# A one-core kernel for grouped attention and a mixture of experts: reordered start and passage, and output products in three fp32r parts from block 15

## The chip, the cores and the metric

The kernel runs on one core of a Trainium2 chip, as one launch. The time is the device time of an execution in microseconds (us). A program of one core has no other core to wait for, so this is its own span and what lies around it.

## What is computed

The reference is one pre-normalised layer on x of 8 sequences x 256 tokens x 256 features, all in fp32: attention with 32 query heads and 8 key heads of width 64, and then 8 experts, of which each token uses its 2 best.

```python
B, S, H = 8, 256, 256
NH, NKV, HD = 32, 8, 64
x = x + attn(layernorm(x))
x = x + moe(layernorm(x))

def attn(h):                       # wq, wk are rotated by rope; causal softmax
    q, k, v = h @ wq.T, h @ wk.T, h @ wv.T
    p = softmax(mask(rope(q) @ rope(k).T / sqrt(64)))
    return (p @ v) @ wo.T

def moe(h):
    val, idx = top_k(h @ gate, 2)
    c = softmax(val)               # weights of the two experts
    for e in idx:                  # w0, w1: 256x512, wo: 512x256
        out += c[e] * ((silu(h @ w0[e]) * (h @ w1[e])) @ wo[e])
```

## The kernel before

**Precision.** A matrix product in plain fp32 takes TensorE (PE) several passes. So the kernel splits most operands into two fp32r tiles, `hi` (the value, cast) and `lo` (value minus `hi`), and adds up three products, hi*hi, lo*hi and hi*lo. ScalarE (ACT) makes `hi`, and VectorE (DVE) makes `lo`. The second product of the experts is an exception: `output` multiplies fp32 tiles, 4 products of 128x256 for a block.

**Attention.** The work goes in 64 turns, `turn(b, g)` for batch b and key head g (a group of 4 query heads). Products of the projections land in the bank `x_bank` ("projected" in rows). ACT and DVE move them out: `rope_q` and `rope_k` on DVE multiply by cosine and sine (`by_cos`, `by_sin`, `k_cos`, `k_sin`), GpSimd (POOL) adds the two ("rotated"), and SyncE (SP) issues the DMAs that put the rotated heads into `kT` and `qT`, 4 for a group (`move_k`, `move_q`). SP also loads the projection weights in 20 pieces into 4 raw slots (`load_piece`); a slot is free again when the piece in it has been split (`split_w` on ACT and on DVE). SP's queue is in order: a load that stands behind a move waits for it. At the start, PE makes keys, then group q0, then q1, all in `x_bank`, so each has to wait until DVE has read the one before.

**Routing.** While attention runs, the gate logits, ranks and slots of the tokens are worked out in small steps on all engines, put between the turns and, for the last two batches, between the blocks (`side_work`). `lane_codes_scaled` (ACT) prepares operands of the `pairs` products (PE); `gap_exp` (ACT) is the exponential of the gates' softmax; `choice_weights` (DVE) uses it.

**Blocks.** The tokens, sorted by expert, make 39 blocks of 128 rows (0 to 38), 17 of them early (`EARLY_BLOCKS`), in which only tokens of the first six batches stand. For block j PE does 6 products for h0, 4 transposes of the block before (tg), 6 products for h1, 2 transposes of the next rows (tx), and the output of the block before (yb). Beside it ACT does silu of h0, a copy of tg into `gT` and a cast of tx into `xsT_hi`, and DVE does `gate_rows` (silu times h1), `x_lo` (`xsT_lo`) and `y_scale` (yb times the gate weight). POOL gathers rows and scatters results by indirect DMA. PE takes the block's expert from the tile `owners` into a register (`owner`).

**Weights of the experts** come by DMA in 8 slots of two halves and are split in place: `slot_hi` on ACT, `slot_lo` on DVE, half by half, by `split_half(j)` in the blocks' side work. Block j waits (`slots_ready`) until the slots that it may use are split. A block's `side_work` on DVE stands ahead of its `y_scale` in DVE's order.

## Time and profile before

| what | value |
| --- | --- |
| time, median of 3 runs (all three) | 809.29 us (806.13, 809.29, 809.66) |
| the profiled execution: its time, its span | 808.83 us, 807.0 us |
| mean granted clock of TensorE | 0.988 |
| busy, share of the span | PE 94%, PEld 80%, DVE 63%, ACT 60%, POOL 53% |
| chain that ended last, by engine | PE 78%, DVE 11%, ACT 4%, issue 4%, DMA 1%, SP's queue 1% |
| its largest lines | h 13%, projections 10%, attn_out 10%, probsT 9%, scores 9%, yb 8% |

An engine is busy while an instruction of it runs; PEld is TensorE loading weights, which overlaps PE. The chain is followed back from the last instruction to what released it, step by step, so it says which work set the time. Rows of it say "start us, us, what"; "issue" is time in which the engine waited for nothing that the profile shows. In a timeline the bracket at the end is the idle time before the instruction and who ended it.

### The profile page before, as it was taken

To read this page: it belongs to the slowest core of one execution; us is meant where nothing else is said; L and a number is where in the kernel's file an instruction comes from. 1 tells how busy PE (TensorE), PEld (TensorE's weight loads), DVE (VectorE), ACT (ScalarE), POOL (GpSimd) and SP (SyncE) were. 2 spreads that over 40 slices of the span, in tenths; PEclk is the share of its full clock that TensorE was granted. 3 is DMA by queue.
4 is the path that set the end of the run, shared out by engine and by line. 5 is a ranking of instruction groups with operands and counts; after the bars stand their busy time and mean duration, and the time that the engine had idled before them with its cause. 6 is when DMAs were issued, how large, how long until landed. Compare 5 with 4: busy or idle time off the path is not lost.

```text
span 807.0 us, 19409 instructions
## 1 busy us (share of the span) xinstructions
PE 756.3 (94%) x5952; PEld 643.5 (80%) x5952; DVE 512.3 (63%) x2117; ACT 480.5 (60%) x1537; POOL 424.3 (53%) x674
## 2 busy tenths in 40 slices
PE   3789999999999999999999999998798999999994
PEld 3678898888888889888888888876587778888883
DVE  5688676767757757766775785888665754333331
ACT  2477877776777777777777767768455432222221
POOL 1365665655655556556565555555324545554442
PEclk9999999999999999999999999999999999999998
DMA  6433123303212130231221213025962233222330
GB/s 204 122 108 105 58 64 73 73 32 76 67 34 61 47 75 33 69 71 35 73 67 38 57 41 76 31 66 152 387 208 40 43 51 50 46 39 43 52 52 6
DMA packets 52852, 61.05 MB, mean 76 GB/s; under 512 B 10545, under 2 KB 45617, under 8 KB 52753
## 3 DMA queue, kind: packets, MB, share of 16 engines
q1 hardware_dynamic: 45264, 50.46, 21.3%
q0 software_dynamic: 7488, 9.36, 6.9%
q8 instruction: 51, 0.84, 0.5%
q14 instruction: 49, 0.39, 0.2%
HBM read 26.21 MB, written 9.32 MB: 44 GB/s over the span
## 4 chain that ended last, share of the span: by engine, by line
PE 78%; DVE 11%; ACT 4%; issue 4%; DMA 1%; SPq 1%; POOLq 0%; POOL 0%; DVEq 0%; ACTq 0%
PE h L1610 13%; PE projected L379 10%; PE attn_out L526 10%; PE probsT L486 9%; PE scores L473 9%; PE yb L1629 8%; PE heads_out L505 6%; PE projected L400 3%; PE heads_out L508 3%; PE projected L357 2%; PE tg L1620 2%; ACT exps L601 1%; ACT exps L599 1%; DMA raw<-w_attn 1%; DVE masked L726 1%
## 5 line engine op out<-in xcount | busy, mean ns | idle before, releaser
L976 POOL TENSOR_SCALAR probs<-exps,inv_sums 128x128 f32<-128x128 f32 x256 | 97.3, 380 | 216.9 <-DVE inv_sums L734 169.7
L608 ACT COPY pT<-probsT 128x384 f32<-128x384 f32 x256 | 121.8, 476 | 82.5 <-PE probsT L486 82.4
L599 ACT ACTIVATE exps<-masked,neg_max 128x128 f32<-128x128 f32 x256 | 103.0, 402 | 54.4 <-DVE neg_max L728 54.2
L486 PE MATMUL probsT<-identity,probs 128*128 128x128 f32 x768 | 130.6, 279 | 5.0 <-ACT pT L608 4.8
L601 ACT ACTIVATE exps<-masked,neg_max 128x256 f32<-128x256 f32 x256 | 127.3, 497 | 0.0
L977 POOL TENSOR_SCALAR probs<-exps,inv_sums 128x256 f32<-128x256 f32 x256 | 125.7, 491 | 0.0
L1832 POOL DMA_INDIRECT out<-y,to_token x39 | 61.9, 1587 | 107.4 <-DVE y L1751 85.2
L379 PE MATMUL projected<-xT_hi,w 128*128 128x256 f32 x512 | 113.6, 302 | 4.9 <-DVE k_sin L716 2.5
L1610 PE MATMUL h<-experts_w,xsT_hi 128*128 x312 | 106.8, 424 | 2.3 <-DVE xsT_lo L1741 1.3
L728 DVE CUSTOM_DVE_ANT_0 masked<-scores,tables 128x256 f32<-128x256 f32 x256 | 107.4, 419 | 0.2 <-issue 0.2
L473 PE MATMUL scores<-kT,qT 64*128 64x128 f32 (+1 forms) x1024 | 102.9, 341 | 2.7 <-DMA qT<-rotated 2.7
L486 PEld LDWEIGHTS probsT<-identity,probs 128*128 128x128 f32 x768 | 88.1, 142 | 18.8 <-issue 11.7
L726 DVE CUSTOM_DVE_ANT_0 masked<-scores,tables 128x128 f32<-128x128 f32 x256 | 71.8, 281 | 47.9 <-PE scores L473 40.2
L962 POOL TENSOR_TENSOR rotated<-by_cos,by_sin 128x512 f32<-128x512 f32 x64 | 84.8, 1325 | 20.2 <-DVE by_sin L705 20.2
L379 PEld LDWEIGHTS projected<-xT_hi,w 128*128 128x128 f32 x512 | 85.9, 195 | 8.8 <-DVE k_sin L716 4.0
L473 PEld LDWEIGHTS scores<-kT,qT 64*128 64x128 f32 x1024 | 73.8, 190 | 16.7 <-issue 10.7
L734 DVE RECIPROCAL inv_sums<-sums 128x2 f32<-128x2 f32 x256 | 41.6, 163 | 67.9 <-ACT exps L601 66.1
L1729 DVE TENSOR_TENSOR raw<-h,raw 128x512 f32<-128x512 f32 x39 | 26.9, 691 | 89.8 <-PE h L1610 85.1
L1688 ACT ACTIVATE raw<-h 128x512 f32<-128x512 f32 x39 | 23.3, 598 | 98.7 <-PE h L1610 98.6
L505 PE MATMUL heads_out<-pT,v_all 128*64 128x256 f32 x512 | 81.2, 396 | 0.6 <-ACT pT L608 0.6
L1629 PE MATMUL yb<-experts_w_out,gT 128*128 x312 | 75.8, 386 | 4.1 <-ACT gT L1693 2.9
L379 PE MATMUL projected<-xT_lo,w 128*128 128x256 f32 x256 | 73.6, 287 | 0.0
(181 smaller groups left out, 1626.3 us busy)
## 6 DMA issues: line engine op xcount, KB each, us to landing
qT<-rotated SPq DMA_DIRECT2D x256, 64.0 KB, 2.2
kT<-k_cos SPq DMA_DIRECT2D x64, 128.0 KB, 3.4
experts_w<-w_in SPq DMA_DIRECT2D x16, 512.0 KB, 7.0
raw<-w_attn SPq DMA_DIRECT2D x20, 256.0 KB, 3.3
experts_w_out<-w_out SPq DMA_DIRECT2D x8, 512.0 KB, 7.7
out<-x_all SPq DMA_DIRECT2D x8, 256.0 KB, 2.3
xn_rows<-raw SPq DMA_DIRECT2D x8, 256.0 KB, 3.9
x_all<-x SPq DMA_DIRECT2D x1, 1792.0 KB, 10.5
```

The lines of the kernel that those rows point to most:

```text
L379: mm = nc.tensor.matmul(x_bank[:, a * SEQ:(a + 1) * SEQ], part[:, at:at + P], x[:, b % 2, k, :], start=(i % 6 == 0), stop=(i % 6 == 5))
L473: mm = nc.tensor.matmul(s_bank[2 * pair + odd][:, tt * SEQ:tt * SEQ + (tt + 1) * P], qT[rows, g % 2, pair, tt * P:(tt + 1) * P], kT[rows, ...
L486: mm = nc.tensor.transpose(p_bank[:, at:at + P], probs[:, h, at:at + P], ident[:, :])
L505: mm = nc.tensor.matmul(o_bank[rows, pair * SEQ:(pair + 1) * SEQ], v, pT[:, n % 2, h, 0:2 * P], start=(pair == 0), stop=False, skip_group_ ...
L599: nc.scalar.activation(exps[:, h, 0:P], masked[:, h, 0:P], ACT.Exp, bias=neg_max[:, h, 0:1], scale=-1.0, accum_out=sums[:, h, 0:1])
L601: nc.scalar.activation(exps[:, h, P:3 * P], masked[:, h, P:3 * P], ACT.Exp, bias=neg_max[:, h, 1:2], scale=-1.0, accum_out=sums[:, h, 1:2] ...
L608: nc.scalar.copy(pT[:, n % 2, h, :], p_bank[:, 0:3 * P]).then_inc(pT_done, 1)
L728: nc.vector.tensor_tensor_reduce(masked[:, h, P:3 * P], s_bank[h][:, SEQ:2 * SEQ], mask[:, 0:2 * P], -(HD ** -0.5), 3e38, ALU.add, ALU.min ...
L976: nc.gpsimd.tensor_scalar(probs[:, h, 0:P], exps[:, h, 0:P], inv_sums[:, h, 0:1], 1.0, ALU.mult, ALU.mult)
L977: nc.gpsimd.tensor_scalar(probs[:, h, P:3 * P], exps[:, h, P:3 * P], inv_sums[:, h, 1:2], 1.0, ALU.mult, ALU.mult).then_inc(probs_done, 1)
L1610: mm = nc.tensor.matmul(ps[:, :], x[:, j % RING, k * P:(k + 1) * P], w[:, bass.ds(expert * 2 * WI + part * WI + (which * KT + k) * MLP, MLP)],
L1629: mm = nc.tensor.matmul(yb[:, 0:EMB], gT[:, k * P:(k + 1) * P], w_out[:, bass.ds(expert * WO + k * EMB, EMB)], start=(k == 0), stop=(k == ...
```

## The change

It has five parts.

- **Start.** PE runs 9 products of the identity with itself ahead of the first transposes and 7 ahead of the keys (`keep_busy`). The groups q0 and q1 are made in two other banks (`y_bank`, "attn_out", and `o_bank`, "heads_out"). Weight pieces 0 and 1 are loaded ahead of the cosine tables. ACT's queue, no longer SP's, issues the 4 moves of the first keys (`move_first_keys`). On DVE, both groups' reads come sooner, among `bn_stats` and splits.
- **Passage from attention to the blocks.** `lane_codes_scaled` goes ahead of two exponentials of the last turn, the turn whose projection is "r" makes its query products whole, a one-element silu is put behind the last turn, and block 0's second half of products goes behind the transposes of block 1.
- **Early blocks.** `gap_exp` goes from the side work of block 4 to that of block 6, `choice_weights` from 5 to 7, and `split_half` leaves out block 6, so that each later half is split one block later.
- **Output from block 15 on.** `output_parts` makes 12 fp32r products of 128x256 from `gT_hi`, `gT_lo`, `second_hi`, `second_lo`. For each such block ACT copies the expert's second weights into `second_hi` (128x1024) and makes `gT_hi`, and DVE makes `second_lo` and `g_lo`, ahead of the next `gate_rows`. The four tiles use space of the attention stage, whose tiles `lane_hot`, `block_codes` and `gT` are moved to the shared stage.
- **Owners.** PE reads the next block's owner behind the fourth h0 product of a block, and works out the next weights' addresses among the h1 products. At the passage to block 17 it waits for the late owners first.

The diff, cut to its core:

```diff
         sp.dma_start(ident[:, :], t["ident"]).then_inc(r["ident_in"], 16)
+        load_piece(0)
+        load_piece(1)
         sp.dma_start(tables[:, :], t["attn_consts"]).then_inc(consts_in, 16)
-        for i in range(SLOTS):
-            load_piece(i)
+        load_piece(2)
+        load_piece(3)
         sp.dma_start(x_all[:, TT:TILES, :], x_dram[:, TT:TILES, :]).then_inc(x_rest_in, 16)
-        move_k(0, 0)
+        move_q(0, 0, True)
         load_piece(SLOTS)
         load_piece(SLOTS + 1)
-        move_q(0, 0, True)
         move_q(1, 1, True)
         for i in range(SLOTS + 2, SLOTS + EARLY):
             load_piece(i)
...
+        def keep_busy(n):
+            for i in range(n):
+                nc.tensor.matmul(s_bank[0][:, 0:P], ident[:, :], ident[:, :], start=True, stop=True)
         pe.wait_ge(r["ident_in"], 16)
+        keep_busy(9)
         x_transposes(0)
+        keep_busy(7)
...
-        project_q(0, 1)
+        project_q(0, 0, bank=y_bank)
+        project_q(0, 1, bank=o_bank)
         batches(turn)
...
+            if (b, g) == (LAST, 7):
+                rt["lane_codes_scaled"](act, 0)
             exponentials(b, g, 2)
             exponentials(b, g, 3)
-            if (b, g) == (LAST, 7):
-                rt["lane_codes_scaled"](act, 0)
             copy_probs(b, g, 0)
             if (b, g) == (LAST, 6):
                 rt["slot_hi"](act, 0, 0)
...
-        for i in range(3):
-            split_w(i)
+            if (b, g) == (LAST, 7):
+                nc.scalar.activation(r["sums"][:, 0, 0:1], r["sums"][:, 0, 0:1], SILU)
+        def move_first_keys():
+            act.wait_ge(k_rotated, 1)
+            for a in range(2):
+                for copy in range(2):
+                    at = copy * HD + a * 32
+                    act.dma_start(kT[at:at + 32, 0, :, :], k_cos[:, a, :]).then_inc(k_in[0], 16)
+        split_w(0)
+        split_w(1)
         x_hi(0)
+        split_w(2)
         split_w(3)
+        move_first_keys()
         split_w(4)
         batches(turn)
         out_hi(LAST, KV_HEADS - 2)
...
         rope_k(0, 0)
+        rope_q(0, True, y_bank)
         split_w(2)
         dve.wait_ge(x_rest_in, 16)
-        for i in range(TT, TT + 4):
+        for i in range(TT, TT + 3):
             nc.vector.bn_stats(stats[:, i, :], x_all[:, i, :])
-        rope_q(0, True)
-        for i in range(TT + 4, TT + 7):
+        rope_q(1, False, o_bank)
+        split_w(3)
+        for i in range(TT + 3, TT + 7):
             nc.vector.bn_stats(stats[:, i, :], x_all[:, i, :])
-        rope_q(1)
-        split_w(3)
         for i in range(TT + 7, TILES):
             ins = nc.vector.bn_stats(stats[:, i, :], x_all[:, i, :])
...
     def split_half(j):
-        return (2 + (j - 1) // 2, (j - 1) % 2) if 1 <= j <= 12 else None
+        n = j - 1 if j < 6 else j - 2
+        return (2 + n // 2, n % 2) if 1 <= j <= 13 and j != 6 else None
...
             pe.wait_ge(gated_done, j + 1)
+            if j > THREE_FROM:
+                pe.wait_ge(gT_lo_done, j - THREE_FROM)
             for k in range(MT):
...
+        def output_parts(j, between=None):
+            i = j - THREE_FROM
+            pe.wait_ge(gT_done, j + 1)
+            pe.wait_ge(second_lo_done, i + 1)
+            pe.wait_ge(y_done, j)
+            n = 0
+            for g, part in ((gT_hi, second_hi), (gT_hi, second_lo), (gT_lo, second_hi)):
+                if n == 2 * MT:
+                    pe.wait_ge(gT_lo_done, i + 1)
+                    if between:
+                        between()
+                for k in range(MT):
+                    mm = nc.tensor.matmul(yb[:, 0:EMB], g[:, k * P:(k + 1) * P], part[:, k * EMB:(k + 1) * EMB],
+                                          start=(n == 0), stop=(n == 3 * MT - 1))
+                    n += 1
+            mm.then_inc(yb_ps, 1)
...
         for j in range(1, BLOCKS):
-            last, expert = owner(j - 1), owner(j)
+            last, expert = expert, following
+            def next_owner(n):
+                nonlocal following
+                if n == 3 and j < LAST and j != EARLY_BLOCKS - 1:
+                    following = owner(j + 1)
...
             pe.wait_ge(gated_done, j)
             slots_ready(j)
-            hidden(j, expert, 0)
+            hidden(j, expert, 0, next_owner)
             g_transposes(j - 1)
-            hidden(j, expert, 1)
+            hidden(j, expert, 1, next_addresses)
             if j < LAST:
                 x_transposes(j + 1)
             outputs_ready(j - 1)
-            output(j - 1, last)
+            if j < LAST:
+                output(j - 1, last)
+            if j == EARLY_BLOCKS - 1:
+                pe.wait_ge(rt["owners_late"], 1)
+                following = owner(j + 1)
             if j == 1:
...
+        def last_transposes():
+            g_transposes(LAST)
+        output_parts(LAST - 1, last_transposes)
+        output(LAST, expert)
...
+            if j >= THREE_FROM:
+                act.wait_ge(yb_ps, j)
+                nc.scalar.copy(gT_hi[:, :], tg[:, :]).then_inc(gT_done, 1)
+                return
             nc.scalar.copy(gT, tg[:, :]).then_inc(gT_done, 1)
+        def second_split_hi(j):
+            if j == THREE_FROM:
+                act.wait_ge(r["pairs_done"], 2)
+                act.wait_ge(rt["owners_late"], 1)
+                for place in range(EXPERTS):
+                    act.wait_ge(r["w_out_in"][place], 16)
+            expert = act.value_load(r["owners"][0:1, j:j + 1], min_val=0, max_val=EXPERTS - 1)
+            act.lower_ap(w_out[:, bass.ds(expert * WO, WO)])
+            act.wait_ge(yb_ps, j)
+            nc.scalar.copy(second_hi[:, :], w_out[:, bass.ds(expert * WO, WO)]).then_inc(second_hi_done, 1)
...
-            if j == 4:
+            if j == 6:
                 rt["gap_exp"](act, 1)
...
             if j < LAST:
                 x_copy(j + 1)
+            if j >= THREE_FROM:
+                second_split_hi(j)
             side_work(j)
         g_copy(LAST)
...
+        def g_lo(j):
+            dve.wait_ge(gT_done, j + 1)
+            nc.vector.tensor_tensor(gT_lo[:, :], tg[:, :], gT_hi[:, :].bitcast(F32), ALU.subtract).then_inc(gT_lo_done, 1)
+        def second_split_lo(j):
+            expert = dve.value_load(r["owners"][0:1, j:j + 1], min_val=0, max_val=EXPERTS - 1)
+            dve.lower_ap(w_out[:, bass.ds(expert * WO, WO)])
+            dve.wait_ge(second_hi_done, j - THREE_FROM + 1)
+            nc.vector.tensor_tensor(second_lo[:, :], w_out[:, bass.ds(expert * WO, WO)], second_hi[:, :].bitcast(F32),
+                                    ALU.subtract).then_inc(second_lo_done, 1)
...
                 rt["both"](dve, 2)
             if j == 5:
-                rt["choice_weights"](dve, 1)
                 rt["late_starts"](dve)
...
                 rt["row_lanes"](dve, 1)
                 rt["row_blocks"](dve, 1)
+                rt["choice_weights"](dve, 1)
             if j == 8:
                 for c in range(2):
                     for part in range(2):
...
         rt["row_newton"](dve, 1, 3)
         rt["row_normalise"](dve, BATCH - 1)
         for j in range(BLOCKS):
+            if j >= THREE_FROM:
+                second_split_lo(j)
+                g_lo(j)
```

**SP's order at the start.** Here `raw<-w_attn` are weight pieces, `x_all` the input, `kT<-k_cos` the moves of the first keys, `qT<-rotated` those of q0 and q1. Before:

```order
L311 DMA tables<-attn_consts 128x1024
L232 DMA raw<-w_attn 128x512 x4
L314 DMA x_all<-x 128x14x256
L254 DMA kT<-k_cos 32x4x256 [waits k_rotated]
L254 DMA kT<-k_cos 32x4x256 x3
L232 DMA raw<-w_attn 128x512 [waits w_split] x2
L243 DMA qT<-rotated 32x2x256 [waits q_rotated]
L243 DMA qT<-rotated 32x2x256 x3
L243 DMA qT<-rotated 32x2x256 [waits q_rotated]
```

After:

```order
L233 DMA raw<-w_attn 128x512 x2
L314 DMA tables<-attn_consts 128x1024
L233 DMA raw<-w_attn 128x512 x2
L317 DMA x_all<-x 128x14x256
L244 DMA qT<-rotated 32x2x256 [waits q_rotated]
L244 DMA qT<-rotated 32x2x256 x3
L233 DMA raw<-w_attn 128x512 [waits w_split] x2
L244 DMA qT<-rotated 32x2x256 [waits q_rotated]
L244 DMA qT<-rotated 32x2x256 x3
```

The four key moves, with the wait for `k_rotated`, have left SP's queue, and the tables stand behind two pieces; q0's moves are the next after the loads.

**ACT's order at blocks 4 to 7.** `experts_w` casts are `slot_hi`, `raw<-h` is silu, `gap` is `gap_exp`. Before:

```order
L1683 CAST xsT_hi<-tx 128x256 [waits xsT_ps]
L1220 ACT_TABLE_LOAD
L1220 ACTIVATE gap<-gap 128x4 [waits gap_done]
L1226 CAST experts_w<-experts_w 128x1024 [waits slot3_half1_in]
L1688 ACT_TABLE_LOAD [waits h0_ps]
L1688 ACTIVATE raw<-h 128x512 [waits gated_done]
L1693 COPY gT<-tg 128x512 [waits gT_ps]
L1683 CAST xsT_hi<-tx 128x256 [waits xsT_ps]
L1226 CAST experts_w<-experts_w 128x1024 [waits slot4_half0_in]
```

After, the rows from silu of block 5 on:

```order
L1777 ACTIVATE raw<-h 128x512 [waits h0_ps,gated_done]
L1786 COPY gT<-tg 128x512 [waits gT_ps]
L1772 CAST xsT_hi<-tx 128x256 [waits xsT_ps]
L1248 CAST experts_w<-experts_w 128x1024 [waits slot4_half0_in]
L1777 ACTIVATE raw<-h 128x512 [waits h0_ps,gated_done]
L1786 COPY gT<-tg 128x512 [waits gT_ps]
L1772 CAST xsT_hi<-tx 128x256 [waits xsT_ps]
L1242 ACT_TABLE_LOAD
L1242 ACTIVATE gap<-gap 128x4 [waits gap_done]
L1777 ACT_TABLE_LOAD [waits h0_ps]
L1777 ACTIVATE raw<-h 128x512 [waits gated_done]
```

The exponential with its two table loads stands two blocks later, in the block in which no half is split; the halves behind it have each moved by one block.

**PE's order in a late block.** `yb` is the output of the block before, `h` the hidden products, `owners` the block's expert. Before:

```order
L1629 ISA
L1629 MATMUL yb<-experts_w_out,gT 128x256
L1629 ISA
L1629 MATMUL yb<-experts_w_out,gT 128x256
L1644 TENSOR_LOAD owners
L1644 ISA x2
L1644 TENSOR_LOAD owners
L1644 ISA x2
L1610 ISA [waits gated_done,xsT_lo_done]
L1610 MATMUL h<-experts_w,xsT_hi 128x512
```

After:

```order
L1694 MATMUL yb<-second_hi,gT_hi 128x256 [waits y_done,second_lo_done,gT_done]
L1694 MATMUL yb<-second_hi,gT_hi 128x256 x3
L1694 MATMUL yb<-second_lo,gT_hi 128x256 x4
L1694 MATMUL yb<-second_hi,gT_lo 128x256 [waits gT_lo_done]
L1694 MATMUL yb<-second_hi,gT_lo 128x256 x3
L1652 MATMUL h<-experts_w,xsT_hi 128x512 [waits gated_done,xsT_lo_done]
L1652 MATMUL h<-experts_w,xsT_hi 128x512
L1652 MATMUL h<-experts_w,xsT_lo 128x512
L1652 MATMUL h<-experts_w,xsT_hi 128x512
L1710 TENSOR_LOAD owners
L1710 ISA x2
L1652 MATMUL h<-experts_w,xsT_hi 128x512
```

Between yb and h the two owner reads and the address instructions are gone; one owner read stands behind the fourth h0 product. The output waits for `second_lo` at its first product and for `gT_lo` at its ninth.

## Rows read from the trace of the kernel before

**Rows 1.** Windows: from:to, length, busy us of each engine, clock, DMA, GB/s.
```profile
10.00:28.00 18.00, 11.66 (x53) 9.98 (x53) 12.26 (x30) 1.76 (x4) 4.58 (x3) 1.00 0.56 156
72.00:560.00 488.00, 480.68 (x4398) 416.45 (x4400) 349.62 (x1591) 357.83 (x1260) 286.29 (x538) 1.00 0.22 59
680.00:720.00 40.00, 40.00 (x203) 33.30 (x202) 12.51 (x37) 11.30 (x24) 20.03 (x17) 1.00 0.27 47
```

**Rows 2.** Chain that ended last, the first 100 us: start us, us, what.
```profile
10.83 2.91 PE projected L357 x12
...
19.49 2.94 PE projected L379 x12
...
23.82 1.66 POOL rotated L962
...
28.01 2.95 DMA raw<-w_attn
...
86.49 1.44 PE attn_out L526 x12
```

**Rows 3.** Timeline of SyncE there: start us, us, queue, line, operation.
```profile
16.89 2.63 SPq L254 DMA_DIRECT2D kT<-k_cos  x4
...
19.57 1.08 SPq L232 DMA_DIRECT2D raw<-w_attn  x2
```

**Rows 4.** Timeline at the passage from attention to the blocks.
```profile
568.04 0.66 ACT L1232 ACTIVATE block_codes<-block_codes,route_tables 128x408 bf16<-128x408 bf16 x1
...
568.84 0.77 PE L1204 MATMUL projected<-block_codes,lane_hot 128*128 128x34 bf16 x24 [2.03 <-ACT block_codes L1232]
...
575.12 1.05 ACT L1226 CAST experts_w<-experts_w 128x1024 fp32r<-128x1024 f32 x1
...
578.91 0.44 PE L1602 MATMUL tx<-identity,xs 128*128 128x128 f32 x2 [0.35 <-DMA xs<-xn_rows,from_token]
```

**Rows 5.** Timeline of ScalarE around block 5.
```profile
610.41 0.20 ACT L1220 ACTIVATE gap<-gap 128x4 f32<-128x4 f32 x1 [2.10 <-DVE gap L1323]
...
611.57 1.28 ACT L1688 ACT_TABLE_LOAD   x1
```

**Rows 6.** Chain that ended last, blocks 1, 5 to 8 and 12.
```profile
586.05 1.65 PE h L1610 x6
...
614.08 3.52 PE yb L1629 x8
...
627.04 1.99 PE yb L1629 x8
...
634.51 1.61 PE h L1610 x6
...
658.03 0.95 issue
```

**Rows 7.** Timeline of a weight split and the next products.
```profile
650.14 1.22 DVE L1518 TENSOR_TENSOR experts_w<-experts_w 128x1024 fp32r<-128x1024 f32 x1
...
650.79 0.72 PE L1610 MATMUL h<-experts_w,xsT_hi 128*128 x2
```

**Rows 8.** Chain that ended last, one late block.
```profile
706.09 1.39 PE h L1610 x6
707.48 0.44 PE tg L1620 x4
...
709.53 1.73 PE yb L1629 x8
```

**Rows 9.** Timeline of VectorE and ScalarE in that block.
```profile
706.27 0.48 DVE L1751 TENSOR_SCALAR y<-yb,row_weight 128x256 f32<-128x256 f32 x1 [0.78 <-PE yb L1629]
...
708.07 0.58 ACT L1693 COPY gT<-tg 128x512 f32<-128x512 f32 x1
...
709.40 0.69 DVE L1729 TENSOR_TENSOR raw<-h,raw 128x512 f32<-128x512 f32 x1 [2.66 <-PE h L1610]
...
710.24 0.42 DVE L1741 TENSOR_TENSOR xsT_lo<-tx,xsT_hi 128x256 fp32r<-128x256 f32 x1
```

71 lines of the change are left out of this document (48 added, 23 removed).

## The prediction

> **What bounds the kernel now.** I read the busy times by window first, then the chain of waits, then the timeline at the places where the chain leaves TensorE.
>
> In the windows PE is the bound nearly everywhere: 480.68 of 488.00 us from 72 to 560, and 40.00 of 40.00 from 680 to 720 [rows 1]. There a gain has to come out of PE's own work. From 10 to 28 PE is busy for 11.66 of 18.00 only.
>
> The chain says why. At the start it goes from the keys (10.83) over the query groups (the second one at 19.49) to POOL's rotation (23.82) and, behind four moves on SP's queue, to a weight piece issued at 28.01 [rows 2]. PE is also slow there: 12 products of 128x256 take 2.94 us, and the 12 of attn_out later take 1.44. The ratio of 2.04 is that of the two levels of the clock (1.2 and 2.4 GHz), although the profile's clock column shows 1.00 for this window; I go by the durations. Before these products PE had stood still or waited.
>
> At the passage to the blocks, the pairs products wait 2.03 us for ACT's block codes [rows 4]. In block 5, ACT waits 2.10 us for the gap and then loads a table for 1.28 [rows 5], and the output behind it takes 3.52 us [rows 6] in place of 1.73 [rows 8]. Block 13 begins behind 0.95 us of "issue" [rows 6].
>
> A late block is gap-free: 706.09 to 711.26 is 5.17 us, of which the output has 1.73 [rows 8].
>
> **The start.** Three edits act on one chain. Identity products keep PE busy ahead of the transposes and the keys; q0 and q1 in own banks don't wait for DVE's reads; the key moves leave SP. The price of an identity product isn't in the trace. The nearest row is yb, 4 fp32 products of 256 columns in 1.73 [rows 8], so 0.43 each, and for 128 columns 0.22, or 0.43 at the lower level. The 16 are 3.5 to 6.9 us of PE in the 10.8 us before the keys, where PE waits for the layer norm. That wait hides them; without it the 7 ahead of the keys would put the keys off by up to 3 us.
>
> My new chain, from those durations: keys at 10.45 (the four transposes ahead of them run faster), for 1.44, to 11.9. DVE's two reads of a group with the hand-overs are 23.82 - 22.43 = 1.39 [rows 2], so keys are read at 13.3 and q0 (made by 13.4) at 14.8. DVE then makes the low part of q1's weights, about 0.7, and q1 runs from 15.5 to 17.0 and is read at 18.35. POOL's rotation of q0 ends at 16.6, that of q1 at 20.05 (1.66 each). SP: q0's four moves 2.63, as the keys' four [rows 3], to 19.2; two pieces, 1.25, to 20.5; q1's moves to 23.1; then the piece that is issued at 28.01 now. So **-4.9**.
>
> Bounds: if PE stays at the lower level, or the freed queue waits for something else, what remains is the 2.63 of key moves less the 1.6 that SP would have waited for q0's rotation, -1.0. If a further group of 12 also runs at the higher level, 1.5 more, -6.4. I take -4.9, since two of the three edits don't need the clock.
>
> The key moves now stand in ACT's queue ahead of a weight split. The Trainium skill speaks against that edit: "DMA: Bandwidth & Descriptors", section "Issuing engines are not separate DMA queues", says that several issuing engines save only a sequencer's time to start a transfer, and that this is usually small. By it the start would gain 3.9. The trace disagrees here: four issues held SP for 2.63 us [rows 3], with loads queued behind them.
>
> **The passage.** With `lane_codes_scaled` ahead of two exponentials the pairs products lose most of their 2.03 wait; but behind them the gathers have to land, since the first tx waits 0.35 for a DMA [rows 4]. Bounds 0 and -2.2. I take -1.2, the middle, because the routing between pairs and gather moves up with the products and the transfer does not get shorter.
>
> **Early blocks.** Without `gap_exp` in block 4's side work ACT's wait goes, -2.1 [rows 5], and the output behind it runs at the rate of the others, 1.73 for 3.52, -1.8 [rows 6, 8]. At block 6 the gap is long there, but silu of block 7 still stands behind a table load of 1.28 [rows 5], against a slack of 0.88 between the end of the copy of gT (708.65) and the output (709.53) [rows 8, 9]: +0.4. `choice_weights` leaves block 5's side work, which ends just ahead of the y that the output at 627.04 waits for [rows 6]: -0.5.
>
> The halves of the weights are split a block later. A low half takes DVE 1.22 and now ends 0.57 after the next block's first product has begun (650.14 + 1.22 against 650.79) [rows 7]; nobody waits there. One block later that block needs it: the second halves of slots 4, 5, 6 and 7 stand in the side work of blocks 7, 9, 11 and 13, and blocks 9, 11, 13 and 15 ask for them. Lateness 0.57 and about 0.2 for loading PE's weights again is 0.75 each. At block 13 the pairs products on PE cover it; three others give +2.25. Bounds 0 and +3.
>
> Owners ahead take away the issue time at 658.03, -0.85 of 0.95. In blocks 7 to 12 the h products take up to 1.65, as 1.61 at 634.51 [rows 6], in place of 1.39 [rows 8]; half of that wait may be the owner's, -0.5 in all. The sum of this part: -2.1 - 1.8 + 0.4 - 0.5 + 2.25 - 0.85 - 0.5 = **-3.1**.
>
> **Late blocks.** 12 fp32r products of 128x256 take 1.44 [rows 2] in place of 1.73, so PE alone would need 5.17 - 0.29 = 4.88. But the loop over DVE is not much shorter: from h's start to `gate_rows` 3.31 (706.09 to 709.40), from there to the end of `x_lo` 1.26 (710.24 + 0.42) [rows 8, 9], then 0.16 to PE, and a start of PE behind a wait costs 0.26 (1.65 [rows 6] against 1.39): 4.99. Addresses made ahead save perhaps some hundredths. I take 4.95: 0.22 x 23 periods (blocks 16 to 38) = **-5.1**. Bounds: 0 (the period stays) and 0.29 x 23 = -6.7.
>
> The new work fits narrowly, counted from the output's end: ACT copies second_hi, 128x1024 as the split at 575.12, 1.05 [rows 4]; DVE scales y in 0.48 beside it [rows 9], then second_lo, as the split of 1.22 [rows 7], to about 2.5; gT is copied by 2.56 (708.65) [rows 9]; g_lo from PSUM, as `gate_rows`, 0.69, to about 3.3, and `gate_rows` starts at 3.31 [rows 9]. So PE doesn't wait; the margin is about 0.05.
>
> **Tail.** Behind the last block nothing covers the second split: second_hi 1.05, second_lo 1.22 and 1.44 of products, and 0.44 for tg [rows 8] ahead of them, with hand-overs 4.5, where now tg, the copy 0.58 and yb 1.73 make 3.2: **+1.3**. If PE falls to the lower level while it waits, 1.4 more.
>
> **Sum.** -4.9 - 1.2 - 3.1 - 5.1 + 1.3 = -13.0, from the profiled execution's 808.83: 795.8. The median of the runs lies 0.46 above that execution: **796.3**.
>
> **Rivals.**
> - Late blocks gain nothing: `gate_rows` stands behind second_lo and g_lo, and with a margin of 0.05 a hand-over of 0.3 more than I count makes DVE's loop 5.17 again. For it: four engines hand over within 3.3 us, and two engines read a register each block. Against: register reads can run ahead of their waits. 796.3 + 5.1 = 801.4.
> - The start gains 1.0 only: PE stays slow, or the moves were hidden behind the splits. For it: the chain behind 28.01 goes on over a DMA of 2.95 [rows 2] and engines that are busy. Against: the queue order frees two things that the chain names. 800.2.
> - The splits' stalls don't come, because DVE has side work to spare there: 794.0. Against: the low half is the first of the side work already, and can't move up.
> - Slower: the late loop grows to 5.70. The place is `gate_rows` behind g_lo. If second_hi waits for the owner's register read on ACT behind the output, as PE's owner read did for 0.95 at block 13 [rows 6], everything behind it moves: 0.75 x 23 = 17.3, 813.5. It decides from 0.74 us a block. Against: the read stands ahead of the wait for the output in ACT's queue.
>
> **Chances.** Forecast 0.55 (own range 792 to 800), late blocks 0.20, start 0.15, no stalls 0.06, slower loop 0.04. Down to the lower bounds of start and late blocks without stalls it is 796.3 - 1.5 - 1.6 - 2.25 = 791, and up, with the late blocks' gain gone and most of the start's, 804. The range is 790 to 804. A measurement of this kernel tells about 0.5%, 4.05 us, from no change. All but the last case lie below 805.2; both misses together reach 805.3. So faster 0.93, same 0.04, slower 0.03.
>
> **What would show it.** Products of the first keys at 1.44 and the seventh piece issued near 23; no wait of 2 us ahead of pairs or of the output of block 5; first products of blocks 9, 11 and 15 waiting about 0.75 for the split; late blocks 4.95 apart, their output 1.44, with PE's idle time ended by `xsT_lo`; a gap of 2.5 us ahead of the last output. I'm wrong if late blocks are 5.17 or more apart, above all with `gate_rows` waiting for g_lo, or if the first turns keep the time they have now.

## The result

The changed kernel takes 799.89 us in the median of five executions (799.02 to 801.77), the kernel before 809.66 (806.13 to 810.9). The ratio is 0.9871, 95% interval 0.985 to 0.9892. That is 9.8 us less, where 13.0 were forecast.

The profiled execution has a span of 798.1 us, 8.9 less. Where they came from is read by following single instructions of both traces. The table has the start of ScalarE's copy `pT` (four a turn; the first of the turn) and of VectorE's `y` (one a block).

| what | before | after | difference |
| --- | --- | --- | --- |
| piece behind q1's moves issued | 28.01 | 22.56 | -5.45 |
| pT of turn 4 | 74.05 | 68.27 | -5.78 |
| pT of turn 8 | 105.96 | 101.06 | -4.90 |
| pT of turn 48 | 441.31 | 436.49 | -4.82 |
| pT of turn 52 | 476.48 | 472.63 | -3.85 |
| pT of turn 60 | 544.28 | 542.03 | -2.25 |
| last pT | 576.50 | 571.98 | -4.52 |
| y of block 0 | 593.07 | 591.50 | -1.57 |
| y of block 14 | 675.06 | 670.74 | -4.32 |
| y of block 36 | 789.01 | 779.08 | -9.93 |
| end of the span | 807.0 | 798.1 | -8.9 |

So the start brought 5.8, the stretch from turn 4 to block 0 gave 4.2 of it back, the blocks up to 14 brought 2.75, the late blocks 5.6, and the end cost 1.1. Of the 4.2, attention lost 0.9 at turn 5, 1.0 at turn 50 and 1.6 at turn 58, and only 0.7 was lost between pT of turn 60 and block 0.

**The start**, in the chain of waits of the changed kernel (start us, us, what):

```profile
7.91 0.66 PE projected L349 x4
8.56 1.56 PE scores L560 x14
10.13 1.59 PE projected L359 x12
11.72 1.45 PE attn_out L381 x12
...
16.25 0.70 SPq L244
...
22.56 2.97 DMA raw<-w_attn
```

The 14 records of L560 are the 7 identity products ahead of the keys, two records each, as yb has; with 1.56 for 7 they take the 0.22 that was estimated. Behind them the keys take 1.59 and q0, in its own bank ("attn_out"), 1.45, where [rows 2] have 2.91 for the keys and 2.94 for q1 (q0, at 15.18, took 2.94 too). SyncE begins q0's moves at 16.25, and the piece of 28.01 is issued at 22.56.

**The passage**, in the timeline of the changed kernel (idle time and releaser in the bracket), then two rows of its chain, and last the gather of block 0's rows in the kernel before:

```profile
565.50 0.75 PE L1226 MATMUL projected<-block_codes,lane_hot 128*128 128x34 bf16 x24 [0.94 <-DVE lane_hot L1482]
...
569.22 1.17 POOL L1945 DMA_INDIRECT xs<-xn_rows,from_token  x1 [0.32 <-issue]
...
576.13 0.44 PE L1636 MATMUL tx<-identity,xs 128*128 128x128 f32 x2 [2.10 <-DMA xs<-xn_rows,from_token]
```

```profile
569.22 6.86 DMA xs<-xn_rows,from_token
...
578.69 2.63 PE h L1652 x6
```

```profile
572.59 1.17 POOL L1822 DMA_INDIRECT xs<-xn_rows,from_token  x1 [0.32 <-issue]
```

Against [rows 4]: the pairs products come 3.3 earlier, of which 2.2 is an earlier attention, and wait 0.94 for 2.03. The gather that follows comes 3.4 earlier too (569.22 for 572.59) and takes 6.86. That is little more than before, where the transposes that wait for it start 6.32 behind its issue; in the 6 us from the issue the DMA engines moved 409 GB/s before and 408 now. What has changed is TensorE's own work beside it. Before, its products behind the wait of 2.03 ran at a granted clock of 0.53 (570 to 573), and its work ended 5.97 behind the gather's issue; now it ends 4.81 behind it. So the transposes wait 2.10 for the gather and not 0.35. Behind that wait the granted clock is 0.50 (577.5 to 580.5), the lower level, and block 0's first six products take 2.63, where a block's take 1.39 [rows 8].

**Early blocks**, every wait of TensorE over 0.5 us from 600 to 676:

```profile
622.11 1.99 PE L1677 MATMUL yb<-experts_w_out,gT 128*128 x8 [0.54 <-ACT gT L1786]
...
629.95 0.70 PE L1652 MATMUL h<-experts_w,xsT_hi 128*128 x2 [0.67 <-DVE experts_w L1542]
...
641.41 0.70 PE L1652 MATMUL h<-experts_w,xsT_hi 128*128 x2 [0.64 <-DVE experts_w L1542]
...
651.25 1.99 PE L1677 MATMUL yb<-experts_w_out,gT 128*128 x8 [0.98 <-issue]
...
665.16 0.71 PE L1652 MATMUL h<-experts_w,xsT_hi 128*128 x2 [0.68 <-DVE experts_w L1542]
```

The wait of 2.1 us and the slow output of block 5 [rows 5, 6] are gone. What is new: 0.54 for gT at block 7 (silu stands behind a table load) and 0.67, 0.64 and 0.68 ahead of blocks 9, 11 and 15, each ended by `experts_w` on VectorE, the low half of a split. Ahead of the output at block 12, 0.98 of issue time stands (0.76 before); the 0.95 ahead of block 13 [rows 6] is gone.

**A late block**, six instructions that follow each other, and a window of 40 us:

```profile
734.67 1.05 ACT L1798 CAST second_hi<-experts_w_out 128x1024 fp32r x1 [1.06 <-PE yb L1694]
...
735.75 1.23 DVE L1861 TENSOR_TENSOR second_lo<-experts_w_out,second_hi 128x1024 fp32r<-128x1024 f32 x1 [0.46 <-ACT second_hi L1798]
...
736.64 0.58 ACT L1784 CAST gT_hi<-tg 128x512 fp32r<-128x512 f32 x1
...
737.25 0.69 DVE L1854 TENSOR_TENSOR gT_lo<-tg,gT_hi 128x512 fp32r<-128x512 f32 x1 [0.28 <-ACT gT_hi L1784]
...
737.97 0.69 DVE L1836 TENSOR_TENSOR raw<-h,raw 128x512 f32<-128x512 f32 x1
...
738.87 0.41 DVE L1848 TENSOR_TENSOR xsT_lo<-tx,xsT_hi 128x256 fp32r<-128x256 f32 x1
```

```profile
671.00:711.00 40.00, 40.00 (x244) 34.58 (x243) 29.13 (x57) 20.51 (x33) 22.89 (x17) 1.00 0.31 52
```

`gate_rows` (737.97) starts right behind `g_lo`, and PE has no idle time: 40.00 of 40.00. The period is 4.92 us for 5.17 [rows 8].

**The end**, y of blocks 37 and 38 after, then the last two scatters of GpSimd after and before:

```profile
784.31 0.48 DVE L1871 TENSOR_SCALAR y<-yb,row_weight 128x256 f32<-128x256 f32 x1 [1.38 <-PE yb L1694]
...
788.42 0.48 DVE L1871 TENSOR_SCALAR y<-yb,row_weight 128x256 f32<-128x256 f32 x1 [1.35 <-PE yb L1694]
```

```profile
785.58 2.32 POOL L1955 DMA_INDIRECT out<-y,to_token  x1 [2.88 <-DVE y L1871]
789.87 1.55 POOL L1955 DMA_INDIRECT out<-y,to_token  x1 [1.97 <-DMA out<-y,to_token]
```

```profile
795.22 1.55 POOL L1832 DMA_INDIRECT out<-y,to_token  x1 [2.94 <-DVE y L1751]
798.73 1.55 POOL L1832 DMA_INDIRECT out<-y,to_token  x1 [1.96 <-DMA out<-y,to_token]
```

The last y comes 4.11 us behind the one before (3.19 in the kernel before). The last scatter waits in both kernels until the one before has landed, and that one took 2.32 to issue for 1.55.

### The profile page after: what moved, and what is told of

The parts are those of the page before. It is cut to its first block, busy times and chain, and to the rows that moved or that the text cites. A ratio compares the mean times of both kernels' runs of the same rounds, so it can differ in the third digit from the quotient of the medians.

```text
span 798.1 us, 19659 instructions
## 1 busy us (share of the span) xinstructions
PE 750.7 (94%) x6080; PEld 642.7 (81%) x6080; DVE 560.4 (70%) x2165; ACT 505.6 (63%) x1562; POOL 430.1 (54%) x674
## 4 chain that ended last, share of the span: by engine, by line
PE 74%; DVE 13%; issue 4%; ACT 4%; DMA 3%; SPq 1%; POOL 0%; POOLq 0%; DVEq 0%; ACTq 0%
PE h L1652 13%; PE attn_out L528 10%; PE projected L381 9%; PE scores L475 9%; PE probsT L488 9%; PE heads_out L507 5%; PE yb L1694 4%; PE projected L402 3%; PE heads_out L510 2%; PE yb L1677 2%; PE tg L1665 2%; PE projected L359 2%; DVE masked L743 1%; DMA xs<-xn_rows,from_token 1%; DVE masked L745 1%
## 5 line engine op out<-in xcount | busy, mean ns | idle before, releaser
L1955 POOL DMA_INDIRECT out<-y,to_token x39 | 69.3, 1778 | 94.2 <-DVE y L1871 51.4
L475 PE MATMUL scores<-kT,qT 64*128 64x128 f32 (+1 forms) x1024 | 105.5, 347 | 4.9 <-DMA qT<-rotated 4.5
L381 PE MATMUL projected<-xT_hi,w 128*128 128x256 f32 x496 | 107.0, 297 | 2.5 <-DVE k_sin L733 1.5
L475 PEld LDWEIGHTS scores<-kT,qT 64*128 64x128 f32 x1024 | 75.2, 193 | 19.5 <-issue 10.8
L381 PEld LDWEIGHTS projected<-xT_hi,w 128*128 128x128 f32 x496 | 80.8, 190 | 6.1 <-DVE k_sin L733 3.0
L381 PE MATMUL projected<-xT_lo,w 128*128 128x256 f32 x248 | 69.9, 282 | 0.0
L1652 PEld LDWEIGHTS h<-experts_w,xsT_hi 128*128 128x128 f32 x312 | 53.9, 191 | 13.7 <-issue 6.4
L756 DVE TENSOR_TENSOR oT_lo<-heads_out,oT_hi 128x512 fp32r<-128x512 f32 x64 | 44.0, 688 | 26.5 <-ACT oT_hi L618 26.4
L1652 PE MATMUL h<-experts_w,xsT_lo 128*128 x156 | 61.7, 396 | 0.0
## 6 DMA issues: line engine op xcount, KB each, us to landing
x_all<-x SPq DMA_DIRECT2D x1, 1792.0 KB, 10.8
```

The costliest lines, as they stand in the source:

```text
L381: mm = nc.tensor.matmul(bank[:, a * SEQ:(a + 1) * SEQ], part[:, at:at + P], x[:, b % 2, k, :], start=(i % 6 == 0), stop=(i % 6 == 5))
L475: mm = nc.tensor.matmul(s_bank[2 * pair + odd][:, tt * SEQ:tt * SEQ + (tt + 1) * P], qT[rows, g % 2, pair, tt * P:(tt + 1) * P], kT[rows, ...
L1652: mm = nc.tensor.matmul(ps[:, :], x[:, j % RING, k * P:(k + 1) * P], first_weights(expert, part, which * KT + k), start=(n == 0), stop=(n ...
```

## The experiments

Each is the changed kernel with the edit that is named. All times stand against runs of the kernel before on the same chip, and positions against the table above. A profile is one execution: those of e1, e7 and e10 are the longest of their runs, those of e2, e5, e6, e8 and e9 the shortest.

Executions of the same code differ at the start already. Nine profiles have the changed start whole. In five of them (the changed kernel, e2, e6, e11, e12) the first four transposes take 0.66 and the piece behind q1's moves is issued at 22.45 to 22.56; in the other four (e3, e4, e5, e10) they take 1.12, about as without identity products (1.09 before), and the piece is issued at 23.66 to 23.88. pT of turn 4 lies between 67.2 and 69.9 in the nine. So a difference of a position between two runs counts only where it is clear of this spread, or is read from one place of a run to another.

| run | median us | ratio to before | 95% interval | span of the profile |
| --- | --- | --- | --- | --- |
| changed kernel | 799.89 | 0.9871 | 0.985 to 0.9892 | 798.1 |
| e1, start as before | 802.77 | 0.9904 | 0.9869 to 0.9939 | 803.9 |
| e2, plain output | 801.7 | 0.9918 | 0.9891 to 0.9944 | 796.5 |
| e3, second weights later | 796.3 | 0.9856 | 0.981 to 0.9902 | 794.3 |
| e4, last block plain | 797.16 | 0.9854 | 0.9812 to 0.9896 | 794.6 |
| e5, splits back | 797.77 | 0.9857 | 0.9828 to 0.9885 | 793.5 |
| e6, exponential back | 800.72 | 0.989 | 0.9865 to 0.9914 | 797.9 |
| e7, no identity products | 802.16 | 0.9894 | 0.9874 to 0.9915 | 803.1 |
| e8, key moves on SyncE | 798.99 | 0.9866 | 0.9844 to 0.9889 | 795.3 |
| e9, shared bank | 800.75 | 0.9885 | 0.9865 to 0.9906 | 797.6 |
| e10, one more VectorE operation | 807.28 | 0.9951 | 0.9933 to 0.9968 | 805.8 |
| e11, best parts | 796.26 | 0.9816 | 0.98 to 0.9833 | 794.5 |
| e12, best parts, "r" in parts | 796.5 | 0.9815 | 0.9789 to 0.9841 | 792.0 |

The intervals of all single edits but e10 overlap that of the changed kernel, so the positions carry those verdicts.

**e1: the start undone.** The order of loads, the banks, the identity products, VectorE's order and the key moves are those of before.

> The changed kernel with the start as before: no identity products, q0 and q1 in the shared bank, the key moves on SyncE's queue, tables loaded first. Theory 1 (the start's gain is kept through attention and comes out at the end): the trace of the changed kernel has the copies of pT 4.85 us earlier than before through turns 12 to 48, so this run is 4 to 5.5 us slower than the changed kernel, about 804.5. Rival (the passage to the blocks absorbs it, since block 0 waits for a gather behind weight transfers whatever attention does): 0 to 2 us slower, and block 0's first products begin near where the changed kernel has them, 578.7.

pT of turn 4 is 5.03 later than in the changed kernel, of turns 8 to 60 4.1, y of block 0 2.4, and the end 5.8, with losses of its own in blocks 2, 5, 9 and 34. The medians are 2.9 apart (2.7 by the ratios), between the two. At y of block 0 the profiles are nearer because this profile does not have the low clock there: from the start of block 0's first product to that of its seventh it takes 1.63, in the changed kernel's profile 2.60. The gather takes 6.1 us from its issue in this run too. By the positions theory 1 holds: y of block 0 is 17.8 behind the last pT, and 17.5 to 18.3 in seven other profiles with the same passage (the changed kernel's 19.5 and e7's 20.2 have the low clock there), so it does not swallow an earlier start. Its own loads start earlier with attention: the five second-weight loads are issued at 565.25 in the changed kernel and at 569.96 here.

**e2: plain output.**

```diff
-THREE_FROM = 15
+THREE_FROM = 39
```

> The changed kernel with the output in 4 plain fp32 products in all blocks, so without the weight and gate splits of late blocks. Theory (the gain of late blocks is PE's own, 0.25 us for each of 22 blocks, and the tail costs 0.9 to 1.3): the period goes back to 5.17, +5.4, the tail back to that of before, -1: 4 to 4.6 us slower, about 804. Rival (the owners made ahead and not the products shortened the period): period 5.0 to 5.1, so 1 to 3 us slower at most.

The last two outputs are written as plain ones with it. The period is 5.17 again in each of blocks 16 to 36 (y of two blocks in a row at 726.78 and 731.95, with 5.17 between all of them), so the 0.25 come with the products, and owners read ahead bring nothing alone; whether the products would bring all of it without them no run shows. From y of block 36 to the end it takes 17.9, as before, and 19.0 in the changed kernel. The median moves by 0.0047 of 810, 3.8 us.

**e3: five second-weight loads later.**

```diff
-                for i in (4, 5, 6):
-                    rt["load_w_out"](sp, i)
...
-        rt["load_w_out"](sp, 2)
-        rt["load_w_out"](sp, 3)
         sp.wait_ge(pT_ps, TURNS * GROUP)
         rt["load_slot"](sp, 4)
         sp.wait_ge(o_ps, TURNS)
         rt["load_slot"](sp, 5)
+        for i in (2, 3, 4, 5, 6):
+            rt["load_w_out"](sp, i)
```

> The changed kernel with five second-weight loads (places 2 to 6) issued behind the loads of slots 4 and 5, so that they are not in the queues when block 0's rows are gathered. Theory (the gather takes 6.9 us because it shares the DMA engines with weights): it lands within 3 to 4 us of its issue, PE's wait of 2.10 ahead of block 0's transposes goes and its first products take 1.4 and not 2.63: 2 to 3.3 us faster, about 797. Rival (the gather is slow by itself): it takes 6 to 7 us again and the time stays within 0.7. Against both: slots 4 and 5 then share the engines with the five loads a little later and a block waits for its weights, slower by some us.

Timeline of this run, gather and first transposes; then the same window of it and of the changed kernel (the last two numbers are the DMA share and GB/s):

```profile
568.10 1.17 POOL L1943 DMA_INDIRECT xs<-xn_rows,from_token  x1 [0.33 <-issue]
...
572.81 0.44 PE L1634 MATMUL tx<-identity,xs 128*128 128x128 f32 x2
```

```profile
566.00:572.00 6.00, 4.33 (x43) 3.42 (x41) 4.46 (x15) 4.25 (x8) 4.11 (x5) 1.00 0.95 354
```

```profile
566.00:572.00 6.00, 4.84 (x51) 3.77 (x46) 4.05 (x17) 4.70 (x10) 3.79 (x7) 1.00 1.03 416
```

With 354 GB/s in place of 416 in that window the gather lands 4.6 after its issue and not 6.9, and PE does not wait for it. y of block 0 is 16.7 behind the last pT, as in the kernel before (16.6), against 19.5 in the changed kernel. That 19.5 is a high one: in eight other profiles with the loads of the changed kernel it is 17.5 to 18.3, in e7 20.2; with the loads of this run it is 16.7, 17.4 (e11) and 16.7 (e12). So the edit is worth about 1 in most executions and not 2.8. The blocks behind give 0.2 back. The theory holds for the wait, though the transfer is still longer than forecast (3 to 4). In e11 it took 5.7, and PE waited 0.98, so the gain is not a fixed one.

**e4: the last block alone with a plain output.**

```diff
+            if j == LAST:
+                nc.scalar.copy(gT_last, tg[:, :]).then_inc(gT_done, 1)
+                return
...
-            if j >= THREE_FROM:
+            if THREE_FROM <= j < LAST:
```

> The changed kernel with the last block's output alone in 4 plain fp32 products, so without its weight and gate splits. Theory (the tail costs the 0.9 us by which the last y now comes later behind the one before, 4.11 against 3.19): 0.9 us faster, last y 3.2 behind the one before. Rival (the end hangs on the scatters, the last of which waits until the one before has landed, 4.3 us after its issue): the last y comes 0.9 earlier, but the end moves by 0.3 at most.

Last two scatters in its timeline:

```profile
782.89 1.55 POOL L1959 DMA_INDIRECT out<-y,to_token  x1 [2.88 <-DVE y L1875]
786.41 1.55 POOL L1959 DMA_INDIRECT out<-y,to_token  x1 [1.96 <-DMA out<-y,to_token]
```

y of block 38 is 2.91 behind that of block 37, and the span ends 13.0 behind y of block 37, for 13.8 in the changed kernel and 13.0 before. The end does hang on the scatter ahead, as the rival has it, and still moves by 0.8: that scatter is issued in 1.55 again, since `second_lo` no longer runs beside it. Each theory had a half of it.

**e5: the splits in the blocks of before**, the exponential still in block 6.

```diff
-        n = j - 1 if j < 6 else j - 2
-        return (2 + n // 2, n % 2) if 1 <= j <= 13 and j != 6 else None
+        return (2 + (j - 1) // 2, (j - 1) % 2) if 1 <= j <= 12 else None
```

> The changed kernel with the halves of the experts' weights split in the blocks of before (1 to 12), the exponential left in block 6. Theory (the later splits cost what the changed kernel's trace shows ahead of blocks 9, 11 and 15: 0.67, 0.64 and 0.68 of waiting for the low half, and 0.26 each for filling PE again): these waits go, 2.0 to 2.8 us faster, about 797.5. Rival (block 6 then has an exponential with two table loads and a split on ScalarE, so silu of block 7 comes later by the split's 1.05): the output at block 7 waits 1 us longer than its 0.54, which leaves 1 to 1.5 faster.

Waits of TensorE over 0.5 us from block 5 to 15:

```profile
618.82 1.99 PE L1676 MATMUL yb<-experts_w_out,gT 128*128 x8 [0.54 <-ACT gT L1785]
...
629.86 0.44 PE L1635 MATMUL tx<-identity,xs 128*128 128x128 f32 x2 [0.64 <-DMA xs<-xn_rows,from_token]
...
647.26 1.99 PE L1676 MATMUL yb<-experts_w_out,gT 128*128 x8 [0.79 <-issue]
```

The three waits for `experts_w` are gone. From y of block 8 to y of block 13 it takes 28.26 us for 30.05, -1.8, and blocks 14 to 17 give 0.5 back: 1.3 net. At block 9 nothing is won, because the transposes there now wait 0.64 for a gather. The rival's longer wait at block 7 doesn't come: it is 0.54 again.

**e6: the exponential back in block 4**, choice weights in 5, splits as in e5.

```diff
-            if j == 6:
+            if j == 4:
                 rt["gap_exp"](act, 1)
```

> The changed kernel with the exponential back in block 4's side work, the choice weights in block 5's and the splits in the blocks of before. Theory (the three moves are -3.9 at block 5, -0.5 at block 6, +0.4 at block 7 and +2.0 to 2.8 at blocks 9, 11 and 15): y of block 4 comes 3.6 later behind y of block 3 than in the changed kernel (7.45 for 3.87), and in all the run is 1.2 to 2 slower, about 801.5. Rival (the low clock of before's output at block 5 was chance): 0 to 0.5 slower, the output there 1.73 again behind its wait of 2.1.

```profile
610.11 2.71 PE L1676 MATMUL yb<-experts_w_out,gT 128*128 x8 [2.04 <-ACT gT L1785]
```

This is its wait of TensorE at block 5. y of block 4 is 2.8 us later behind y of block 3 than in the changed kernel, where 3.6 were expected, and y of block 8 is 3.8 later: the forecast's -3.9 with its two small terms. The output at block 5 takes 2.71 here and took 3.52 before [rows 6], for 1.99 of the output at 627.04 [rows 6] and 1.73 in a late block [rows 8]; the granted clock is 0.51 from 611.2 to 614.0 here, and 0.55 from 614.0 to 617.6 before. Both profiles with the wait of 2.0 to 2.1 have the low clock behind it, and the output is longer by a different amount in each, so the rival's 1.73 is out.

**e7: no identity products.**

```diff
-        keep_busy(9)
         x_transposes(0)
-        keep_busy(7)
```

> The changed kernel without the 16 identity products at the start. Theory (they only raise PE's clock for the first products): keys 2.9 for 1.59, q0 2.9 for 1.45, so q0 is moved 2 to 2.8 us later, the piece behind q1's moves is issued 2 to 3 us later, and the time is 2 to 3 longer, about 802. Rival (moves on SyncE's queue set the start, not products): the piece is issued at 22.6 as now, the time stays within 0.7.

```profile
10.46 2.90 PE projected L359 x12
...
25.39 2.79 DMA raw<-w_attn
```

In its chain the keys take 2.90 again, and the piece is issued at 25.39, 2.8 later than in the changed kernel and still 1.5 later than the latest of the nine. pT of turns 4 to 60 is 3.1 later, at turn 4 clear of the nine by 1.6. The theory holds.

**e8: the key moves on SyncE.**

```diff
-        move_first_keys()
...
+        move_k(0, 0)
         move_q(0, 0, True)
```

> The changed kernel with the 4 moves of the first keys on SyncE's queue again, ahead of q0's. Theory (four issues hold the queue for 2.63 us, of which q0's rotation covers 1.6): q0's moves and all behind them, the piece issued at 22.56 too, come 1 to 1.3 later, and the time is about 1 longer, 801. Rival (an issuing engine saves nothing that lasts, since transfers share the same engines): within 0.3, the piece issued at 22.6 and the first scores where they are.

```profile
14.39 0.70 SPq L255
...
17.06 0.60 SPq L244
...
23.25 2.87 DMA raw<-w_attn
```

Its chain goes over the key moves (14.39), q0's moves begin at 17.06 for 16.25, and the piece is issued at 23.25, 0.7 later; its transposes take 0.66, and the five profiles with that have the piece at 22.45 to 22.56. pT of turns 4 to 56 is 0.6 later, which is within the spread of the nine, and the time does not show it (ratio 0.9866). So the move of four issues to another engine is worth about 0.7 at the piece, between theory and rival; that any of it comes out at the end is not shown.

**e9: q0 and q1 in the shared bank**, each behind VectorE's reads.

```diff
+        pe.wait_ge(k_parts, 1)
-        project_q(0, 0, bank=y_bank)
-        project_q(0, 1, bank=o_bank)
+        project_q(0, 0)
+        pe.wait_ge(q_parts, 1)
+        project_q(0, 1)
...
```

> The changed kernel with q0 and q1 made in the shared bank again, each behind VectorE's read of the group before; identity products, key moves on ScalarE's queue and VectorE's order stay. Theory (the start's gain has three parts: identity products 3.1 and key moves 0.7 by the runs without them, so own banks have the rest of the 5.0): pT of turn 4 comes 1.0 to 1.5 later than in the changed kernel, 69.5, and the time is 1 to 1.5 longer. Rival (q1 waits for the low part of its weights on VectorE in either case, so banks are worth nothing): within 0.3 at turn 4.

```profile
10.54 1.62 PE projected L359 x12
...
13.60 1.71 PE projected L381 x12
...
24.67 2.92 DMA raw<-w_attn
```

Keys end at 12.16 and q0 begins at 13.60: 1.4 of waiting. The piece is issued 2.1 later, and pT of turns 4 to 56 is 2.07 later, of which 0.4 is a later beginning of the keys (10.54 for 10.13): its transposes take 1.11. From the end of the keys to the piece it takes 12.5, for 10.8 in the five profiles with transposes of 0.66 and 11.2 to 11.5 in the four others. So banks are worth 1.1 to 1.7, about what was expected.

**e10: one more VectorE operation in each late block.** Its result is not used.

```diff
             dve.wait_ge(gT_done, j + 1)
+            nc.vector.tensor_tensor(extra, tg[:, :], gT_hi[:, :].bitcast(F32), ALU.subtract)
```

> The changed kernel with one more VectorE subtraction of 128x512 from PSUM, 0.69 us, ahead of g_lo in each of the 24 late blocks; its result is not used. Theory (gate_rows stands right behind g_lo, so late blocks have next to no room on VectorE): the period grows by 0.5 to 0.75, from 4.92 to 5.4 to 5.7, 11 to 16 us in all, about 812 to 816, with PE waiting for xsT_lo. Rival (PE is the bound with room to spare, as it is busy all the time): less than 3 us slower.

Timeline of one late block of it (the first row is the added operation):

```profile
741.26 0.69 DVE L1855 TENSOR_TENSOR raw<-tg,gT_hi 128x512 f32<-128x512 f32 x1 [0.59 <-ACT gT_hi L1785]
...
741.87 0.68 DVE L1856 TENSOR_TENSOR gT_lo<-tg,gT_hi 128x512 fp32r<-128x512 f32 x1
...
742.47 0.68 DVE L1837 TENSOR_TENSOR raw<-h,raw 128x512 f32<-128x512 f32 x1
...
743.14 0.42 DVE L1849 TENSOR_TENSOR xsT_lo<-tx,xsT_hi 128x256 fp32r<-128x256 f32 x1
...
743.62 0.73 PE L1653 MATMUL h<-experts_w,xsT_hi 128*128 x2
```

The period is 5.22, 0.30 more, and the time 6.5 us longer by the ratios. Neither theory: of the added 0.69, 0.39 is covered. `gate_rows` starts 0.60 behind the start of `g_lo` and not 0.72, and `xsT_lo` 0.67 behind `gate_rows` and not 0.90. In the changed kernel both had short waits of their own there (for h1 and for `xsT_hi`), and these take up a delay of `g_lo`.

**e11 and e12: the best parts together.** Splits of e5, loads of e3, the last block of e4, and the last transposes behind the output of block 37; e12 also makes the query products of turn "r" in two parts again.

> The changed kernel with the splits in the blocks of before, five second-weight loads behind slots 4 and 5, and a tail with a plain fp32 output of the last block and its transposes behind the output before. Theory (each part adds what its own run showed: 1.3 at the splits, 1 to 2.8 at the gather, 0.8 to 1.1 at the end): 3 to 5 us faster than the changed kernel, 795 to 797. Rival (the parts cover the same wait): no faster than the best of them alone, about 797.

> The run before with the query products of turn (7,2), the one whose projection is the ranks, in two parts again, as in the kernel before. Theory (the whole product leaves PE nothing to do behind it, and in three of nine profiles the scores that follow ran at the lower level of the clock, 1.6 us more): those scores take 1.6 and never 2.3 or 2.9, and the time is up to 0.8 less in the median. Rival (the level there goes by chance and the order has no part in it): no difference beyond 0.5.

e11 is 0.9816 of the kernel before, its interval is clear of the changed kernel's: 4.5 us less by the ratios, within the expected 3 to 5. e12 is the same, and in its profile one group of scores of the last turns runs slowly as well (2.24 us from first to last start, the granted clock 0.50), so the order of turn "r" doesn't decide on that.

## Why the prediction was right, and where it was off

- **Start, -4.9 forecast, -4.8 to -5.8 measured.** The chain of the prediction came out almost to the number (piece at 23.1, measured 22.56, and 22.45 to 23.88 in the nine profiles). The shares did not: I wrote that "two of the three edits don't need the clock" and gave the key moves 1.0. At the piece, identity products have 1.5 to 2.9 (e7), banks 1.1 to 1.7 (e9), key moves 0.7 (e8); together 3.3 to 5.3, each read from one profile, where the whole start has 5.2 (e1's piece is issued at 27.75). By the Trainium skill ("DMA: Bandwidth & Descriptors", "Issuing engines are not separate DMA queues") the moves to another engine should win little. With 0.7 of a 2.63 us issue time in the chain, and nothing that the time shows, this case does not speak against it.
- **Attention, nothing forecast, +2.6 measured** (from turn 48 to turn 60). This is the largest miss: the sum has no term for attention and carries the start's gain through it whole. At turn 50, 1.0 was lost, in ten of the twelve experiments too, and at turn 58 1.6, in seven of the twelve (below). The kernel before has neither in its one profile; whether its other executions have them is not shown.
- **Passage, -1.2 forecast, +0.7 in the profile from pT of turn 60 to y of block 0.** It takes 48.8 there before and 49.5 in the changed kernel's profile. But nine experiments have the same code there (all but e3, e11 and e12): eight of them take 47.5 to 48.2, and e7 50.1. So most executions have a gain of 0.6 to 1.3, as forecast, and the profiled one is one of the two that lose, with the low clock in block 0. What the bounds of 0 and -2.2 left out is a loss. That "behind them the gathers have to land" was right: in all profiles 3.7 lie between the pairs products and the gather's issue, and the gather takes 6.3 more before and 5.9 to 7.8 with these loads. Against the products ahead of the pairs, this chain came forward by the 1.1 that the pairs' wait lost, and TensorE's work up to the gather by 2.3. So TensorE now waits 1.1 to 3.1 for the gather in all ten profiles with these loads. e3 shows that the second-weight loads lengthen the gather.
- **Early blocks, -3.1 forecast, -2.75 measured** (81.99 us from y of block 0 to y of block 14, then 79.24). The exponential was right (e6: 3.8), the wait for gT at block 7 too (0.54, forecast 0.4). The splits' stalls came at the three blocks named and with the size named, 0.67, 0.64 and 0.68; undone, they bring 1.3 and not 2.25, since a gather is late at block 9 anyway and blocks 14 to 17 give 0.5 back. The rival without stalls is out. What the owners read ahead bring here, 1.35 in the sum, no run measured by itself.
- **Late blocks, -5.1 forecast, -5.6 measured.** Period 4.92 for 4.95. The bound is PE's products and not, as I took it, VectorE's loop at 4.99; the margin of 0.05 was 0.39 (e10). With that the slower rival was further off than I had it, and so was the one without gain.
- **Tail, +1.3 forecast, +1.1 measured** (17.9 to 19.0 from y of block 36). The term was for y of block 38, which does come 0.9 later; what counts is the scatter of block 37 (e4).

Start, late blocks, early blocks and tail are within 1 us of their terms. The median of the runs is 3.6 us above the forecast; in its profile the sum is missed by 4.1, of which 2.6 are the losses in attention and 1.9 the passage. The range of 14 us was wide enough for both, but it was not made for a loss in attention, and that the time lies inside the narrower 792 to 800 by 0.1 is luck.

## What to carry to other kernels

Follow a gain at the start of a kernel to its end, in more than one execution: single waits on the way can take some of it back. Where the next stage hangs on a transfer, less work of TensorE beside the transfer turns into waiting; look at what the transfer hangs on and at what else is in the DMA queues. Where an engine must wait early, a few products without use that raise TensorE's clock can be worth more than a freed queue (e7 against e8). When an off-path engine gets new work, look at the waits in its order as well as its busy time: short waits behind it are room.

## What the runs showed that I had not expected

**VectorE and GpSimd in each other's way.** At turn 50 a small VectorE operation took 1.42 us in the changed kernel and 0.24 before (before first, then after):

```profile
454.27 0.24 DVE L1316 TENSOR_TENSOR hot<-route_tables,code 128x80 f32<-128x80 f32 x1
454.31 1.35 POOL L967 TENSOR_TENSOR k_cos<-k_cos,k_sin 128x512 f32<-128x512 f32 x1
```

```profile
449.45 1.42 DVE L1338 TENSOR_TENSOR hot<-route_tables,code 128x80 f32<-128x80 f32 x1
449.48 1.29 POOL L984 TENSOR_TENSOR k_cos<-k_cos,k_sin 128x512 f32<-128x512 f32 x1
```

In both, GpSimd's `k_cos` begins within 0.04 us of it. The rows start in the same order, yet in the second it is VectorE that runs 1.2 longer, and q's products behind it come 1.0 later. Ten of the twelve experiments' profiles have it; those of e2, e4 and the kernel before don't. At turn 5 the same happens to a weight split: 1.87 us in the changed kernel, while in e4 the split takes 0.69 and `k_cos` 1.79. The Trainium skill ("SBUF — State Buffer", "Who interferes with whom") says that a VectorE instruction with two SBUF inputs contends with a GpSimd instruction that reads SBUF, and that the order of issue decides which of the two is blocked. The durations agree with the first: at turn 5 one or the other is longer, by 1.2 or by 0.5. The second the rows can't show, since VectorE's row starts first in both cases. At turn 50 it starts 0.041 to 0.044 ahead of `k_cos` in the three profiles without the loss and 0.030 to 0.036 in ten with it; but in e1 it is 0.044 with the loss. So hundredths of a us may decide on 1 us, which is not shown.

GpSimd's scatters, issued beside VectorE's new splits, also became longer: 1.78 us in the mean for 1.59, 2.32 for the one of block 37. In e2, without these splits, the mean is 1.59 again.

**TensorE's clock fell in short idle times, but not each time.** In the changed kernel the ranks' products at 522.15 wait 1.79 us for VectorE, and the scores behind them take 2.86:

```profile
522.15 0.51 PE L1199 MATMUL projected<-both,squares 128*128 128x96 bf16 x12 [1.79 <-DVE by_sin L722]
```

```profile
523.18 2.86 PE scores L475 x16
```

In the kernel before the same wait of 1.79 stands ahead of the same products, and the scores take 1.58. The wait is 1.78 to 1.81 in all profiles, and the granted clock behind it is 0.50 in the changed kernel (523 to 526) and in seven of the experiments, and 1.00 in the other five and before. From pT of turn 58 to pT of turn 60 the eight take 18.5, the others 16.9. At block 0 the low clock came behind the waits of 2.10 and 3.09 (e7) for the gather, and not behind those of 1.1 to 1.9 in the other eight with these loads. What decides between them stays open.
